# One-hot adjacency shared between VectorE and ScalarE, and weight loads of 128 columns in a graph and mixture-of-experts network

## What is computed

```python
x = normal(1250, 512)
src = randint(20000,) in 0..1249
dst = (1250 * uniform(20000,) ** 2).astype(int)      # many edges point to low nodes
order = argsort(dst); src, dst = src[order], dst[order]

xn = layernorm(x)
# graph part of layer 0, others alike:
h = xn @ W.T + b
out = segment_sum(norm[:, None] * h[row], col)        # = A^T-like product with a 1250x1250 adjacency
# mixing part of layer 0, twice:
data_dash = einsum('bhnd,md->bhnm', data * normalizer, proj)     # 256 features of each head
diag = sum(data ** 2, -1, keepdims=True) * 0.5 * normalizer ** 2 # squares of each head
kp = exp(data_dash - diag - max) + eps
# expert parts of layers 0, 2 and 3:
logits = x @ gate_w.T                                  # 8 gates of each node
```

## Time and profile before

| | |
|---|---|
| median of 3 runs | 3042.52 us (3034.19 to 3045.39) |
| profiled execution | 3037.47 us |
| its span | 3035.7 us, 46375 instructions |
| PE busy | 2654.5 us, 87% of the span |
| PEld busy | 1730.4 us, 57% |
| DVE busy | 1719.0 us, 57% |
| ACT busy | 1133.8 us, 37% |
| POOL busy | 1218.9 us, 40% |
| adjacency, first matmul to last tile's end | 12.34 to 161.10 us |

### The profile page before, as it was taken

How to read it: one execution, slowest core, us unless ns; L and a number is a source line. 1 busy time by engine, 2 the same in 40 slices (tenths; PEclk the granted TensorE clock), 3 DMA queues, 4 the chain that set the end, 5 groups by cost and what they waited for, 6 DMA issues and landing times. The chain is left out here.

```text
span 3035.7 us, 46375 instructions
## 1 busy us (share of the span) xinstructions
PE 2654.5 (87%) x16989; PEld 1730.4 (57%) x16989; DVE 1719.0 (57%) x3474; ACT 1133.8 (37%) x2528; POOL 1218.9 (40%) x1469
## 2 busy tenths in 40 slices
PE   7999889999988999989898976999599969669684
PEld 4655659556556855555554645777346646445452
DVE  8876778734687863766535353222436366564743
ACT  3254457423546633322412232444332325432141
POOL 2021577776277778855404222111004226410042
PEclk9999899999999999989998987999899969979797
DMA  2001355433044544424101008999601049720298
GB/s 65 1 20 62 105 152 157 131 123 101 32 135 145 162 123 125 124 88 126 42 4 42 28 20 343 414 415 415 218 1 43 29 148 333 243 58 1 69 362 267
DMA packets 164805, 415.35 MB, mean 137 GB/s; under 512 B 24027, under 2 KB 75771, under 8 KB 141356
## 3 DMA queue, kind: packets, MB, share of 16 engines
q1 hardware_dynamic: 150077, 362.10, 35.3%
q0 software_dynamic: 12960, 42.48, 3.7%
q10 hardware_dynamic: 1555, 7.95, 1.1%
HBM read 325.37 MB, written 87.09 MB: 136 GB/s over the span
## 5 line engine op out<-in xcount | busy, mean ns | idle before, releaser
L2859 POOL TENSOR_SCALAR raw<-raw 128x512 f32<-128x512 f32 x376 | 265.4, 706 | 987.2 <-PE ps L510 305.4
L528 PE MATMUL ps<-units,ARENA 128*125 128x512 f16 x2760 | 613.0, 383 | 14.7 <-POOL units L2863 9.8
L510 PE MATMUL ps<-ARENA,units 128*128 128x500 f16 (+1 forms) x2952 | 541.9, 346 | 22.1 <-ACT tmp L1480 6.8
L528 PEld LDWEIGHTS ps<-units,ARENA 128*125 128x125 f16 x2760 | 373.0, 138 | 239.8 <-DVE X L2513 16.4
L510 PEld LDWEIGHTS ps<-ARENA,units 128*128 128x128 f16 x2952 | 289.8, 99 | 272.3 <-issue 25.9
L1913 DVE TENSOR_TENSOR ARENA<-tmp,ARENA 128x500 f16<-128x500 f32 (+3 forms) x237 | 167.4, 712 | 391.8 <-ACT ARENA L1406 200.1
L2863 POOL TENSOR_TENSOR AT<-raw,AT 128x512 f16<-128x512 f32 x200 | 244.1, 1220 | 17.0
L2863 POOL TENSOR_TENSOR units<-raw,units 128x512 f16<-128x512 f32 x188 | 231.2, 1230 | 16.0
L1405 ACT ACTIVATE tmp<-ps,cols 128x500 f32<-128x500 f32 (+1 forms) x144 | 87.6, 608 | 355.7 <-PE ps L510 348.4
L2912 POOL DMA_INDIRECT picks_d<-ARENA,proj x81 | 82.2, 1015 | 344.1 <-DVE ARENA L2356 343.8
L1002 PE MATMUL ps<-ARENA 128*128 128x128 f16 x3240 | 192.3, 220 | 1.8 <-DVE ARENA L2347 1.6
(11 more groups left out here) (471 smaller groups left out, 4519.7 us busy)
## 6 DMA issues: line engine op xcount, KB each, us to landing
ARENA<-split_d SPq DMA_DIRECT2D x135, 1024.0 KB
raw<-in_moe SPq DMA_DIRECT2D x200, 256.0 KB, 3.0
split_d<-AT SPq DMA_DIRECT2D x200, 256.0 KB, 2.5
raw<-in_units SPq DMA_DIRECT2D x188, 256.0 KB, 2.6
ARENA<-split_d SPq DMA_DIRECT2D x27, 1280.0 KB
rows_d<-ARENA SPq DMA_DIRECT2D x6, 896.0 KB
ARENA<-picks_d SPq DMA_DIRECT2D x6, 896.0 KB
ARENA<-picks_d ACTq DMA_DIRECT2D x6, 896.0 KB
```

Source lines behind the costliest of these rows:

```text
L510: ins = pe.matmul(o[:, 0:nt * R], wt, mv_, start=(i == 0), stop=(i == len(steps) - 1))
L528: ins = pe.matmul(o[0:R, :], th(srcT, h, k, t, 1), w(k, g), start=(i == 0), stop=(i == len(steps) - 1))
L2859: pool.tensor_scalar(r, r, WEIGHT_SCALE, gain, ALU.mult, ALU.mult).then_inc(sem("pool_step"), 1)
```

## The change

It has five parts.

1. **Every second target one-hot is made ahead, on ACT.** A node's row inside its tile does not depend on the tile of the loop, so 81 one-hots for the odd slots are made once and kept in `odd_slots` (in the space of `Y`): `Abs(row - iota)`, then `Relu(1 - that)`, in batches of 1, 1, 2, then 4. PE waits for them by a semaphore `onehot_odd` against a register's value and reads them at a register's address.
2. **Sources are masked per tile.** Since a target one-hot now tells only the row inside a tile, DVE sets the source of each edge that is not of the current tile to zero (numbers now begin with one) by one operation on 125x160 ahead of each tile, in two buffers. Three operations ahead of the first tile make `tile_of` and `row_in_tile`.
3. **Finer spans.** A tile's span begins at any row of 250 edges, and its count is rounded up to whole groups of four slots.
4. **First norm later.** ACT's sums, squares and rows stand behind its copies of tiles 1, 2 and 3.
5. **Wide weight loads.** `head_pair`, `token_rows` and `gate_tiles` load 128 columns in place of 125 where three more exist to be read: always in `head_pair`, in 8 of 10 tiles in `token_rows`, in 7 of 10 in `gate_tiles` (all but tiles 3, 7 and 9). The rows 125 to 127 of the output are read by nobody.

```diff
+ODD_BATCHES = [1, 1, 2] + [4] * 19 + [1]
+ROUND = 1.5 * 2.0 ** 23
...
+        def th_wide(buf, part, k, t):
+
+            a = (part * KC + k) * N + t * R
+            return halves[buf][:, a:a + (128 if t + 1 not in CHUNK_STARTS and t + 1 < T else R)]
+
+        def stack_wide(h, t, wide=128):
+
+            return halves["K"][:, h * N + t * R:h * N + t * R + wide]
...
+                first = pe.value_load(span_i[0][:, dt:dt + 1], min_val=0, max_val=EROWS - 1)
                 groups = pe.value_load(span_i[1][:, dt:dt + 1], min_val=1, max_val=GROUPS)
                 before = pe.value_load(span_i[2][:, dt:dt + 1], min_val=0, max_val=T * GROUPS)
                 with pe.Fori(0, groups) as it:
                     for j in range(EH_SLOTS):
+                        rows = ohd[j][:, 0:R]
+                        if j % 2 == 1:
+                            odd = first + it * 2 + j // 2
+                            pe.wait_ge(sem("onehot_odd"), odd + 1)
+                            rows = odd_columns[:, bass.ds(odd * 128, R)]
                         pe.wait_ge(sem("onehot"), (before + it) * EH_SLOTS + (j + 1))
                         for b, (a0, a1) in enumerate(SPAN):
-                            ins = pe.matmul(psA[b][0:R, 0:a1 - a0], ohd[j][:, 0:R], ohs[j][:, a0:a1], start=False, stop=False)
+                            ins = pe.matmul(psA[b][0:R, 0:a1 - a0], rows, ohs[j][:, a0:a1], start=False, stop=False)
...
-                        ins = pe.matmul(o[0:R, h2 * NBF:(h2 + 1) * NBF], stack(2 * hp + h2, t, 1), features(dep, part),
+                        ins = pe.matmul(o[:, h2 * NBF:(h2 + 1) * NBF], stack_wide(2 * hp + h2, t), features(dep, part),
...
-                        ins = pe.matmul(o[0:R, h * DH:(h + 1) * DH], stack(h, t, 1), sum_halves[:, :], start=True, stop=True)
+                        n = 128 if t + 1 not in CHUNK_STARTS else R
+                        ins = pe.matmul(o[0:n, h * DH:(h + 1) * DH], stack_wide(h, t, n), sum_halves[:, :], start=True, stop=True)
...
-                        ins = pe.matmul(o[0:R, t * 16:t * 16 + 16], th("YT", 0, k, t, 1), gates16[:, :, at_ + k * 8:at_ + k * 8 + 8],
+                        ins = pe.matmul(o[0:th_wide("YT", 0, k, t).shape[1], t * 16:t * 16 + 16], th_wide("YT", 0, k, t), gates16[:, :, at_ + k * 8:at_ + k * 8 + 8],
...
+            act.wait_ge(sem("edge_tables"), 3)
+            odd = 0
+            for n in ODD_BATCHES:
+                for i in range(odd, odd + n):
+                    ins = act.activation(odd_slots[:, i * 128:(i + 1) * 128], iota16[:, 0:128], ACT.Abs, bias=row_in_tile[:, 2 * i + 1:2 * i + 2], scale=-1.0)
+                ins.then_inc(sem("act_step"), s.one("act_step"))
+                act.wait_ge(*s.latest())
+                act.activation(odd_slots[:, odd * 128:(odd + n) * 128], odd_slots[:, odd * 128:(odd + n) * 128], ACT.Relu, bias=ones[0:R, 0:1], scale=-1.0).then_inc(sem("onehot_odd"), n)
+                odd += n
...
                 adjacency_nat(dt)
+                if dt == 1:
+                    first_sums()
+                if dt == 2:
+                    first_squares()
+                if dt == 3:
+                    first_rows()
...
+            dve.wait_ge(sem("edgesT"), s.more("edgesT", 2))
...
+            then(ts(tile_of, edgesT[1], -0.5 * (R + 1), 1.0 / R, ALU.add, ALU.mult))
+            then(ts(tile_of, tile_of, ROUND, -ROUND, ALU.add, ALU.add))
+            stt(row_in_tile[:, 0:EC], tile_of, -float(R), edgesT[1], ALU.mult, ALU.add).then_inc(sem("edge_tables"), s.one("edge_tables"))
...
             for dt in range(T):
-                first = dve.value_load(span_i[0][:, dt:dt + 1], min_val=0, max_val=GROUPS - 1)
+                then(stt(src_in_tile[dt % 2][:, 0:EC], tile_of, float(dt), edgesT[0], ALU.is_equal, ALU.mult))
+                first = dve.value_load(span_i[0][:, dt:dt + 1], min_val=0, max_val=EROWS - 1)
...
                         dve.wait_ge(sem("onehot_used"), (before + it) * EH_SLOTS + (j + 1))
-                        c = (first + it) * EH_SLOTS + j
-                        ts(ohs[j][:, 0:N], iota16, edge_columns[0][:, bass.ds(c, 1)], None, ALU.is_equal)
-                        ts(ohd[j][:, 0:R], iota16[:, dt * R:(dt + 1) * R], edge_columns[1][:, bass.ds(c, 1)], None,
-                           ALU.is_equal).then_inc(sem("onehot"), 1)
+                        c = (first + it * 2) * 2 + j
+                        ins = ts(ohs[j][:, 0:N], iota16, src_columns[dt % 2][:, bass.ds(c, 1)], None, ALU.is_equal)
+                        if j % 2 == 0:
+                            ins = ts(ohd[j][:, 0:R], iota16[:, 0:R], row_columns[:, bass.ds(c, 1)], None, ALU.is_equal)
+                        ins.then_inc(sem("onehot"), 1)
```

More of the change, by code:

```diff
@@ L248, in build @@
         edgesT = [K[0:R, 1000 + i * EC:1000 + (i + 1) * EC] for i in range(2)]
-        edge_columns = [K[0:R, 1000 + i * EC:1000 + i * EC + 2 * EC] for i in range(2)]
+        tile_of = K[0:R, 3900:3900 + EC]
+        row_in_tile = K[0:R, 4060:4060 + EC + 2]
+        src_in_tile = [K[0:R, 4222 + i * (EC + 2):4222 + (i + 1) * (EC + 2)] for i in range(2)]
+        src_columns = [K[0:R, 4222 + i * (EC + 2):4222 + i * (EC + 2) + 2 * EC] for i in range(2)]
+        row_columns = K[0:R, 4060:4060 + 2 * EC]
+        odd_slots = Y[0:R, 0:(EROWS + 1) * 64].bitcast(F16)
+        odd_columns = ARENA[0:R, sum(ARENA_WIDTHS[:3]):sum(ARENA_WIDTHS[:3]) + (EROWS + 2 * GROUPS - 1) * 64].bitcast(F16)
         a_nat = [K[0:R, 1400 + i * N:1400 + (i + 1) * N] for i in range(2)]
@@ L1500, in _ @@
                 act.activation(edgesT[e].rearrange("p (r h) -> p h r", h=2), o[0:R, 0:EC].rearrange("p (h r) -> p h r", h=2),
-                                      ACT.Copy).then_inc(sem("edgesT"), s.one("edgesT"))
-            act.wait_ge(sem("x_loaded"), s.more("x_loaded", 16 * len(PARTITION_CUTS)))
-            for t in range(T):
-                ins = act.activation(nat(M, t), nat(X, t), ACT.Identity, accum_out=std[0:R, t:t + 1])
-            ins.then_inc(sem("act_step"), s.one("act_step"))
@@ L1506, in _ @@
-            act.wait_ge(*s.latest())
-            act.activation(mv[0:R, :, 0], std[0:R, :], ACT.Identity, scale=-1.0 / D).then_inc(sem("act_step"), s.one("act_step"))
-            act.wait_ge(*s.latest())
-            for t in range(T):
-                ins = act.activation(nat(M, t), nat(X, t), ACT.Square, bias=mv[0:R, t, 0:1], accum_out=std[0:R, t:t + 1])
-            ins.then_inc(sem("squares"), s.one("squares"))
-            act.wait_ge(*s.latest())
-            act.wait_ge(sem("ln_scales"), s.more("ln_scales", 1))
@@ L1514, in _ @@
-            for t in range(T):
-                act.activation(nat(M, t), nat(X, t), ACT.Identity, bias=mv[0:R, t, 1:2], scale=rstd[0:R, t:t + 1]).then_inc(sem("normed"), s.one("normed"))
+                                      ACT.Identity, bias=ones[0:R, 0:1]).then_inc(sem("edgesT"), s.one("edgesT"))
+            act.wait_ge(sem("edge_tables"), 3)
[7 more added lines that the diff above has]
+                odd += n
@@ new lines, in first_sums @@
+            def first_sums():
+                act.wait_ge(sem("x_loaded"), s.more("x_loaded", 16 * len(PARTITION_CUTS)))
+                for t in range(T):
+                    ins = act.activation(nat(M, t), nat(X, t), ACT.Identity, accum_out=std[0:R, t:t + 1])
+                ins.then_inc(sem("act_step"), s.one("act_step"))
+                act.wait_ge(*s.latest())
+                act.activation(mv[0:R, :, 0], std[0:R, :], ACT.Identity, scale=-1.0 / D).then_inc(sem("act_step"), s.one("act_step"))
+                act.wait_ge(*s.latest())
@@ new lines, in first_squares, with first_rows @@
+            def first_squares():
+                for t in range(T):
+                    ins = act.activation(nat(M, t), nat(X, t), ACT.Square, bias=mv[0:R, t, 0:1], accum_out=std[0:R, t:t + 1])
+                ins.then_inc(sem("squares"), s.one("squares"))
+                act.wait_ge(*s.latest())
+            def first_rows():
+                act.wait_ge(sem("ln_scales"), s.more("ln_scales", 1))
+                for t in range(T):
+                    act.activation(nat(M, t), nat(X, t), ACT.Identity, bias=mv[0:R, t, 1:2], scale=rstd[0:R, t:t + 1]).then_inc(sem("normed"), s.one("normed"))
@@ L1965, in _ @@
             dve.tensor_reduce(bounds[0], edges_f[1], AX_X, ALU.max)
-            dve.tensor_reduce(bounds[1], edges_f[1], AX_X, ALU.min).then_inc(sem("row_bounds"), s.one("row_bounds"))
+            dve.tensor_reduce(bounds[1], edges_f[1], AX_X, ALU.min).then_inc(sem("edge_tables"), s.one("edge_tables"))
             dve.memset(ones[:, :], 1.0)
+            dve.memset(ARENA[:, sum(ARENA_WIDTHS) - 2:sum(ARENA_WIDTHS)], 0.0)
             dve.memset(EPS_LN, LN_EPS)
```

44 lines of the change are left out of this document (23 added, 21 removed).

## The result

The changed kernel takes 3017.77 us (median of 7 runs, 3013.59 to 3024.39), the kernel before 3042.52 (7 runs on the same chip, 3031.43 to 3049.17). The ratio is 0.9934, 95% interval 0.9918 to 0.9950: 15 to 25 us less. The prediction was 3013. The profiled execution took 3017.77 us, its span 3016.0, so 19.7 us less than the span of before.

A forecast was written before the change was run, and what follows sets the result against it. DVE's one-hots were taken to pace the adjacency, with PE the bound from tile 2 on after the change. 11.6 (adjacency) + 5.9 (squares) + 6.9 (gates) = 24.4 off 3037.47 gave 3013 us, range 2999 to 3034.

The forecast's parts named there:

- Adjacency: Opening stage: odd one-hots leaving DVE, fewer groups and moved POOL splits gain 2.7 + 4.1 + 1.9 + 0.8 + 2.1 = 11.6 us.
- one register load more on PE: Head of each adjacency tile on PE: 0.25 us for the added load, so a tile costs 3.3 us.
- POOL: Weight splits move from 34 to about 86 us; 4.7 of the 6.8 us stolen from DVE come back, worth 2.1.
- Odd slots at a register's address: PE's weight reads in odd adjacency slots: taken as 0 us extra, hidden behind 0.52 us of matmuls.
- Wide loads: 128-column weight loads in squares and gates: 0.03 us each, gaining 5.9 us in squares and 6.9 in gates.
- The gates: Gate matmuls that DVE waits for: first block gains 2.3 us, second and third 2.3 each, together 6.9.
- The key squares: Squares of the keys on a busy PE: 0.038 us saved on each, 2.4 us a layer, 4.9 in two.
- The queries: Squares of the queries, which wait for ACT's evictions: 1 us gained in all.
- Slower: Rival: register-addressed weight loads drain PE's queue at each of 96 odd slots; 3071 us, chance 0.07.
- odd slots: Rival: odd slots cost PE 0.16 us a pair, the adjacency keeps about 1.5 us; 3023 us, chance 0.10.
- narrow loads gain nothing: Rival: wide loads gain nothing on the path, by a matmul floor or late waiters; 3025 us, chance 0.07.
- given back: Rival: half the gain goes in expert layers that wait for DMA and POOL; 3026 us, chance 0.11.

The follow-up runs named there:

- pe_sum: The changed kernel with PE adding up its third register value from the last tile's instead of loading it; ratio to the kernel before 0.9920.
- adj_only: The changed kernel with narrow weight loads of 125 columns, so the new adjacency and later norm alone; ratio to the kernel before 0.9969, 9 us.
- timed gates: The kernel before with 128-column weight loads in the gate matmuls alone; ratio to the kernel before 0.9972, 8.5 us.

## Why the prediction was right

The total was right and its terms were not all of the right size.

**Adjacency, predicted 11.6, 4.3 at its end.** The term that was mis-sized is the 3.3 us of a tile, the 3.0 between tiles plus "one register load more on PE" at 0.25. A group costs 2.08 us as predicted (0.52 a slot), but a tile costs about 3.9: 12.30 us for tile 3 less 16 x 0.522. Of the 0.6 too little, `pe_sum` gives 0.2 to the load (0.48 in the mean of seven tiles, not 0.25); 0.1 to 0.4 are there with two loads already and were not separated, and 0.14 lie between the last slot and the sums, which the 3.0 left out. The 0.25 was a quarter of DVE's idle time of 1.0, in which three loads and a loop start were perhaps partly covered. The row with the open price was already there, 2.52 us before DVE's very first one-hot. By tiles: tile 0 lost 0.6 against the forecast, tile 1 0.9 (its switch took 2.7 instead of 1.8; with the mask ahead of the loads it is 0.9 less), tiles 2 to 4 2.0 beside the contention, tiles 5 to 9 2.9, and 5.4 us of contention came back instead of 4.7. That is the 7 us. Of these, taking PE's third load away gave 3.3 in tiles 2, 3 and 5 to 9, and DVE's order 0.3 at the start and 0.9 in tile 1. The last tile's end moved by 4.3, 1.2 and, with both, 7.9 us, but tile 0's pace and tile 4's contention, which no edit aimed at, are in those figures. `adj_only` as a whole gains 9 us, nearer to the 11.6 than the adjacency's end is; that part of its gain has no row, so it doesn't confirm the term.

**POOL.** Right in kind and nearly in size. I had it as a benefit of 2.1; the useful question, where these operations cost nothing, was not asked. Behind the last tile they cost nothing that a row shows.

**Odd slots at a register's address.** Free inside a tile, as taken: 55 ns on the weight queue, hidden.

**Wide loads, predicted 12.8.** The gates gave 7.2 by rows (6.9 predicted), and of their second and third waits 2.49 and 2.44 us went, all there was (2.3 each in the forecast). The key squares gave 2.4, not 4.9: the narrow matmul cost 0.054 and not 0.068, a figure that I had from 1.16 us over 16 loads. The first of these loads stands 0.21 us ahead of the first square (327.19 and 327.40), behind the last 512-column matmul; without that, the 15 distances are 0.054 each. The queries gave up to 2.9 instead of 1, the features 0. Together some 12.5. The rival with a floor of some 0.06 us a matmul is refuted: the distance of the gates halves with 128 columns. On that point the Trainium skill (TensorE: Matmul & The Clock Gate, Weight-path perf modes — Fast Weight Load (FWL) and DoubleRow) has the better sentence, the fast load when the number of weights is 128; the 0.0255 us of the gates at 128 columns against 0.057 at 125 agree with it.

**The sum.** 4.3 + 2.4 + 2.9 + 7.2 is 17 us, against 19.7 between the two profiled executions and 15 to 25 by the medians. The forecast's 24.4 reached the median's 24.7 partly by luck: two terms were too large by 10, and 3 to 8 us of the measured difference have no term. Of the wide loads' terms, only the gates' and the features' were tested by timed kernels of their own. Of the prediction's signs, PE's pairs at 1.04 us without idle time, the long one-hots near 90 us and the shorter gates came; the last tile's end near 150 and tile 1 at 14.7 didn't (156.76 and 15.56).

**The rivals.** "Slower" and "odd slots" fall by PE's rate; "narrow loads gain nothing" by the timed gates; "given back" by the adjacency-only kernel, which keeps its gain.

## What to carry to other kernels

Before a register load is added to a loop's head, look for a row where the same loads stand in the open; a value that is a running sum can be kept in a register instead. When operations of POOL slow DVE, ask at what time DVE's work is not awaited and put them there. Make weights exactly 128 columns wide wherever narrow matmuls follow one another and someone waits for the last.

## What the runs showed of the hardware

- A narrow matmul with 128 weight columns starts 0.0255 us after the last one, with 125 columns 0.057 (gates, granted clock 1.00).
- One register load in the open costs PE 0.24 to 0.6 us a tile (`pe_sum`). On DVE three loads and a loop start behind a semaphore wait hold it 2.37 us.
- PE's first slots come 1.04 us apart, twice the later 0.52, at a granted clock of 1.00 in the rows; this stretch lasts 2.6 to 6.1 us from PE's first slot, differently in two executions of one program.
- Beside POOL's splits DVE's 125x125 one-hot takes 0.59 to 1.15 us instead of 0.25, while one of 1250 columns goes from 0.54 to about 0.9: in proportion the small operation suffers most. POOL's subtract takes 1.26 to 1.46 us beside DVE and 1.15 alone.
